# Last layer of a four-layer kernel: the two routed rows of a token are added by GpSimd in SBUF, and TensorE transposes the sum

## The reference, cut to what matters

```python
gu = x @ shared_gate_up_w.T
g, u = jnp.split(gu, 2, axis=-1)
shared = jax.nn.silu(g) * u @ shared_down_w.T          # inner width 704
shared = jax.nn.sigmoid(x @ shared_gate_w.T) * shared
top_w, top_i = jax.lax.top_k(softmax(x @ gate_w.T), 2)  # 2 of 8 experts for each token
top_w = top_w / top_w.sum(-1)
...
ye = jnp.einsum('tei,ehi->teh', he, w2)                 # each expert's result, inner width 176
out = jnp.einsum('teh,te->th', ye, combine) + shared    # combine holds top_w
```

## Time and profile before

| what | us |
|---|---|
| three timed runs, median | 943.83 |
| lowest and highest of them | 941.01, 951.21 |
| the profiled execution, its own time | 939.95 |
| span of that execution, first to last instruction | 938.1 |
| TensorE busy in the span | 830.6 (89%) |
| VectorE, ScalarE, GpSimd busy | 568.6, 345.0, 349.3 |

### The profile page before, as it was taken

One profiled execution on the slowest core, in us unless ns is written; L12 is line 12 of the kernel. 1 busy time (PEld: TensorE's weight loads), 2 busy tenths in 40 slices (PEclk: granted clock), 3 DMA queues, 4 the chain that ended last, 5 costly groups with the idle time before them and its releaser, 6 DMA issues.

```text
span 938.1 us, 16409 instructions
## 1 busy us (share of the span) xinstructions
PE 830.6 (89%) x5234; PEld 665.6 (71%) x5234; DVE 568.6 (61%) x1668; ACT 345.0 (37%) x945; POOL 349.3 (37%) x357
## 2 busy tenths in 40 slices
PE   1999999886898999687578999999979979999997
PEld 1787877654688999586467888866457747777786
DVE  5555888565376887358768999572534344443343
ACT  3333443333232333112367888521543222221211
POOL 7300345446655676676423320000373003334000
PEclk9999999897899999799699999999989989999999
DMA  9326111777986644453788888000623003331232
GB/s 353 75 91 180 40 53 42 252 246 220 256 222 215 178 128 117 179 207 119 142 177 180 188 181 247 4 1 10 199 103 113 19 23 107 101 95 58 90 92 88
DMA packets 62563, 126.37 MB, mean 135 GB/s; under 512 B 17105, under 2 KB 41002, under 8 KB 59840
## 3 DMA queue, kind: packets, MB, share of 16 engines
q1 hardware_dynamic: 45007, 77.85, 28.1%
q0 software_dynamic: 16960, 45.35, 16.9%
q10 hardware_dynamic: 512, 2.13, 1.0%
HBM read 87.39 MB, written 43.30 MB: 139 GB/s over the span
## 4 chain that ended last, share of the span: by engine, by line
PE 59%; DVE 15%; DMA 8%; issue 5%; ACT 4%; SPq 4%; POOL 3%; DVEq 0%; POOLq 0%; ACTq 0%
PE ps L471 19%; PE ps L808 10%; PE ps L839 7%; PE ps L818 3%; DVE early L1975 2%; DMA big<-big 2%; DVE work L1969 2%; PE ps L2300 2%; DVE early L1963 2%; PE ps L829 2%; PE ps L2561 2%; DMA mid<-sent_d 2%; PE ps L2606 2%; POOL sent_d L910 2%; PE ps L2435 2%
## 5 line engine op out<-in xcount | busy, mean ns | idle before, releaser
L910 POOL DMA_INDIRECT sent_d<-mid,slot_i x88 | 98.2, 1116 | 115.0 <-DVE mid L630 65.5
L852 ACT ACTIVATE early<-ps 128x256 f32<-128x256 f32 x134 | 51.3, 384 | 175.7 <-PE ps L818 175.7
L839 PE MATMUL ps<-early 96*128 (+1 forms) x346 | 98.7, 386 | 0.2
L870 DVE TENSOR_TENSOR early<-early,ps 128x96 f32<-128x96 f32 (+1 forms) x134 | 37.3, 278 | 94.9 <-ACT early L858 76.2
L901 POOL DMA_INDIRECT back_d<-early,mid x78 | 77.2, 989 | 38.9 <-issue 27.2
L505 DVE TENSOR_TENSOR hidl<-work,hidh 128x512 fp32r<-128x512 f32 (+1 forms) x56 | 38.7, 691 | 85.0 <-ACT hidh L498 85.0
L511 ACT ACTIVATE work<-ps 128x512 f32<-128x512 f32 (+1 forms) x56 | 33.4, 596 | 140.7 <-PE ps L471 140.5
L808 PE MATMUL ps<-big,early 128*128 x380 | 81.3, 337 | 3.8 <-ACT early L852 1.6
L901 POOL DMA_INDIRECT back_d<-big,mid x39 | 38.4, 984 | 112.0 <-DVE big L884 107.5
L808 PEld LDWEIGHTS ps<-big,early 128*128 128x128 f32 x380 | 69.0, 197 | 10.9 <-issue 5.8
L471 PE MATMUL ps<-yhigh,l_high 128*128 128x512 f32 x128 | 55.2, 432 | 3.9 <-DVE ylow L1712 3.1
(11 more groups left out here) (438 smaller groups left out, 2014.6 us busy)
## 6 DMA issues: line engine op xcount, KB each, us to landing
mid<-sent_d SPq DMA_DIRECT2D x117, 130.0 KB
big<-back_d SPq DMA_DIRECT2D x8, 512.0 KB
mid<-back_d SPq DMA_DIRECT2D x8, 512.0 KB, 6.9
early<-back_d SPq DMA_DIRECT2D x16, 256.0 KB, 3.4
early<-early SPq DMA_DIRECT2D x18, 176.0 KB
big<-big SPq DMA_DIRECT2D x18, 176.0 KB
early<-in_w SPq DMA_DIRECT2D x3, 1024.0 KB, 11.7
big<-in_gate SPq DMA_DIRECT2D x1, 3072.0 KB, 11.4
```

The costliest lines, as they stand in the source:

```text
L839: last = nc.tensor.matmul(ps[:, 6 + j % 2, 0:D], L.hTb[j % len(L.hTb)][0:f1 - f0, h * P:(h + 1) * P], L.down[0:f1 - f0, h, bass.ds(owners[ ...
L852: nc.scalar.activation(L.yTb[b % ring_y], ps[:, b % 2, 0:2 * P], ACT.Copy).then_inc(s["turn_sb"], 1)
L870: nc.vector.tensor_tensor(L.hb[j % ring_h], L.sgb[j % 2], ps[:, 2 + j % 2, F:2 * F], ALU.mult)\
L910: nc.gpsimd.indirect_dma_start(out=sent_d, out_offset=bass.IndirectOffsetOnAxis(ap=L.slot_i[:, i:i + 1], axis=0), in_=L.rows[c][:, t, n, : ...
```

## The change

GpSimd gets 16 adds behind its last scatter, one for each tile, 128 x 256, in place in `gback3`. It waits once for the four loads of a chunk. TensorE's wait moves from the loads (`back0`, `back1`, once for each chunk) to the adds (`had`, once for each tile), and its 16 accumulating matmuls of a chunk (4 tiles x 2 halves x 2 results, against the identity) become 8 transposes (4 tiles x 2 halves). Nothing else moves: `merged`, the loads of SP and their waits are the same.

```diff
@@ gpsimd
             for b in range(NB3):
                 pool_block(pool, L3, b)
+            for c in range(NCH):
+                pool.wait_ge(s["back%d" % (c % 2)], 16 * TPC * (c // 2 + 1))
+                for i in range(c * TPC, (c + 1) * TPC):
+                    rows = gback3[i % GRING3]
+                    nc.gpsimd.tensor_tensor(rows[:, 0:D], rows[:, 0:D], rows[:, D:2 * D], ALU.add).then_inc(s["had"], 1)
@@ combine3(c)
-                pe.wait_ge(s["back%d" % (c % 2)], 16 * TPC * (c // 2 + 1))
                 for t in range(TPC):
                     i = c * TPC + t
+                    pe.wait_ge(s["had"], 1 + NT + i + 1)
                     for d in range(KD):
-                        for k in range(K3):
-                            last = nc.tensor.matmul(ps[:, 4 + d, t * P:(t + 1) * P],
-                                                    gback3[i % GRING3][:, k * D + d * P:k * D + (d + 1) * P], ident,
-                                                    start=(k == 0), stop=(k == K3 - 1))
+                        last = nc.tensor.transpose(ps[:, 4 + d, t * P:(t + 1) * P],
+                                                   gback3[i % GRING3][:, d * P:(d + 1) * P], ident)
                     last.then_inc(s["turn_ps"], 1)
```

## The result

The changed kernel took 929.37 us as the median of four runs (925.02 to 932.68), against 943.5 for the kernel before, now of four runs as well (941.01 to 951.21): a ratio of 0.987, with a 95% interval of 0.983 to 0.991 (the two medians alone would give 0.985). The forecast was 934.0 with a range of 929 to 941, a gain of 9.85 us; the medians lie 14.1 us apart, and 929.37 is only 0.37 inside the lower end of the range.

A forecast was written before the change was run, and what follows sets the result against it. The prediction took TensorE's own work to bound the last 39 us. Four shorter groups save 9.96 us, less 0.11 for a wait: 943.83 - 9.85 = 934.0 us, range 929 to 941.

The forecast's parts named there:

- TensorE alone sets the tail: From 900.87 to the final gate at 931.97, TensorE runs without a gap, so its own time is the span's time.
- A group of 1.00 us: Each of four combine3 groups falls from 3.49 us to 1.00 as 8 transposes, saving 9.96 us in all.
- Waits for each tile cost nothing when met: TensorE waits five times a chunk in place of two; a wait already met was to cost nothing.
- Adds of 0.68 us, hidden: GpSimd's 16 adds of 128x256 take 0.68 us each, all under TensorE: price 0, at worst 1.8 us.
- What becomes late next: At the last piece's down, TensorE arrives at T + 3.95, waits for the low part until T + 4.06, losing 0.11 us.
- T: The start of combine3(3), the last chunk's final group, at 923.83 us in the kernel before.
- The sum: 9.96 - 0.11 = 9.85 us off the whole kernel: 943.83 to 934.0 us, 1.04% less.
- Late adds: Rival: the adds of chunks 2 and 3 reach TensorE late, costing 2.5 us with the lock, 936.5 us; 8%.
- The clock: Rival: transposes let TensorE's clock fall from the first group on, 72 later matmuls cost 14.4 us more, 948.4 us; 4%.
- Two passes: Rival: transposes run two passes, group 1.75 us, gain 6.9, 936.9 us; 4% together with other smaller gains.
- Lock of VectorE and GpSimd: VectorE's low parts in chunks 2 and 3 can be 0.68 us late beside GpSimd's adds; cost 0, up to 0.7.

The follow-up runs named there:

- adds alone: Against the changed kernel, GpSimd's adds and TensorE's waits for them stay, but TensorE does the old 16 accumulating matmuls; tail 31.10 us.
- The first comparison: The changed kernel, no further edit, against the kernel before, four runs each: 929.37 against 943.5 us, ratio 0.987.
- The three comparisons of this kernel: The unedited changed kernel against the kernel before, in the first result and two repeats in later sets: ratios 0.987, 0.9905 and 0.9897.
- the plain matmuls: Against the changed kernel, ordinary fp32 matmuls with the identity replace the transposes and the adds stay; tail 23.95 us, ratio 0.991.

## Why the prediction was right, point by point

- *TensorE alone sets the tail.* Shown: adds alone left 31.10 us, and removing them left 20.59 (one trace each). The gain is TensorE's passes.
- *A group of 1.00 us.* Mis-sized: it cost 0.79. The rows that I took it from the earlier trace rows are followed by an ordinary fp32 matmul and came after an idle gap. What counts is the distance to the next start: there it was 0.07 us less than the group's duration (1.09 and 1.02), here 0.24 less (1.03 and 0.79), just as in the old group (3.73 and 3.49). That 0.24 from the earlier trace rows, taken off the 1.09 of the earlier trace rows, would have given 0.85. Nearer still was a row of the kernel before that I overlooked, eight passes of 128x128 with the very neighbour that the new group has, 867.59 - 866.78 = 0.81 us:

```profile
866.78 1.05 PE L2623 MATMUL ps<-late,sig 128*128 128x128 f32 x8
867.59 0.48 PE L471 MATMUL ps<-yhigh,sguh 128*128 128x512 f32 x1
```

  The term is 4 x 0.21 = 0.84 us too small in gain.
- *Waits for each tile cost nothing when met.* Held: no gap before any group.
- *Adds of 0.68 us, hidden.* They took 0.73 to 1.20, with a median of 0.74, inside both ends of the bound. Hidden they were; but the room was 0.9 us a chunk, not 3. Three sizes went wrong, all one way: chunk 2's adds began 903.73 - 897.31 = 6.4 us behind the start of the group that frees the buffers, where I had put 905.8 - 900.7 = 5.1; the four took 3.3 us and not 2.7; and the group of chunk 2 came 10.0 us behind that of chunk 0, and not 10.4. That the waits were still met is in part luck.
- *What becomes late next.* The last down at T + 4.06 came exactly. With the shorter group TensorE was ready at T + 3.74, so the loss was 0.32 and not 0.11.
- *The sum.* 4 x (3.49 - 0.79) - 0.32 = 10.48 gives, with the sizes measured afterwards, the measured 10.49. The forecast was 9.85, as the group mis-sized by 0.84 and the wait by 0.21 partly cancelled. The first comparison, 13.8 us in the profiles and 14.1 in the medians, held 3.4 us and more that the change does not explain; they took 929.37 to the edge of the range, and that it stayed inside is luck. The three comparisons of this kernel, 0.987, 0.9905 and 0.990, average 0.989, and 943.5 less 10.5 is 0.989 of it.
- *The rivals.* Late adds: not seen, and with adds of 1.1 us apiece the tail was still 20.65. The clock: the granted clock was 1.00 from 897 to 917 in the changed kernel, and the sixfold transposes left it there. Two passes: the plain matmuls did that and cost 3.36 us of gain, near the 2.95 reckoned (9.85 against 6.9).
- *Lock of VectorE and GpSimd.* Longer times of this kind occurred, 0.33 us on a low part of chunk 2 and 0.46 on an add, each hidden as forecast; the low parts of chunk 3 kept their 0.69. The Trainium skill (SBUF — State Buffer, "Who interferes with whom") says that a VectorE instruction with two SBUF inputs contends with a GpSimd instruction that reads SBUF. The trace agrees: in the earlier layer four VectorE adds took 4.88 us beside GpSimd's and 1.43 without them.

## What to carry to other kernels

Where TensorE both transposes and sums rows that lie in SBUF, its passes are what to count: an accumulating fp32 matmul against the identity costs two for each term, a transpose one for all of them, and the sum is free on an idle engine as long as its adds end before TensorE arrives. Price a group by the distance to the start of the very neighbour that it will have, not of one elsewhere. And a sum moved to an engine that is itself waited for may only move the wait: nearly the same edit, with the sum on VectorE beside a busy GpSimd, gave nothing in the earlier layer, where TensorE's clock stayed low as well while it waited for each tile.

## What the runs showed of the hardware that I had not expected

- The granted clock stayed at 1.00 through four runs of 5.24 us of transposes. The Trainium skill (TensorE: Matmul & The Clock Gate, "Part 4: PE-mode transpose") says that a transpose does not count for the clock as a matmul does; the trace shows no effect of it on a clock that is at 1.00. Whether transposes raise a low clock is not shown: in the earlier layer it stayed at 0.50 through pairs of them, but with idle time ahead of each pair.
- An fp32 transpose of 128x128 in a run costs 5.24 / 48 = 0.109 us, a pass of an fp32 matmul 3.57 / 32 = 0.112: a transpose is one such pass.
- When GpSimd adds 128x512 and VectorE 128x256 in turn in SBUF, a tile takes 1.37 to 1.42 us, where GpSimd's alone take 1.28.
- The changed kernel took 929 us in the first comparison and 978 and 982 in two others, with its tail the same to 0.06 us and the stretch from the shared branch of chunk 2 on the same to 0.07: what differs between the sets lies ahead of it.
